# Attention scores computed two steps ahead instead of one, over three score banks, with three side banks instead of four

## The reference, cut to what matters

```
def _spatial_experts(xn, idx, in_w, in_b, out_w, out_b):
    ...
    att = jax.nn.softmax(jnp.einsum('bthd,bshd->bhts', q, k), axis=-1)
    o = jnp.einsum('bhts,bshd->bthd', att, v).reshape(B, T, D)
def _temporal_experts(xt, idx, qw, qb, kw, kb, vw, vb, pw, pb):
    ...
    logits = jnp.where(causal, logits, -jnp.inf)
    att = jax.nn.softmax(logits, axis=-1)
def _cross_mha(q_in, kv_in, in_w, in_b, out_w, out_b):
    ...
```

## Time and profile before

| | |
|---|---|
| median of 3 runs | 1999.56 us (1993.12 to 1999.69) |
| the profiled execution, its own time | 1993.96 us |
| its span, first to last instruction | 1992.2 us |
| mean granted TensorE clock | 0.977 |
| attention passes, in that span | 516 to 1712 us |

### The profile page before, as it was taken

The page is one execution under the profiler, slowest core; times in us unless marked ns, Lnnn a source line. Parts: engine busy times, 40 slices in busy tenths (PEclk is TensorE's granted clock), DMA queues, the critical chain, the costliest instruction groups (busy, mean ns, idle before and its releaser), DMA issues.

```text
span 1992.2 us, 30956 instructions
## 1 busy us (share of the span) xinstructions
PE 1824.9 (92%) x10475; PEld 1625.9 (82%) x10475; DVE 1181.7 (59%) x2333; ACT 723.5 (36%) x1345; POOL 356.4 (18%) x345
## 2 busy tenths in 40 slices
PE   1899989976899999999999899989999999999998
PEld 0678657864799989989888898879999999788996
DVE  6577558775556546563746657556656566576332
ACT  0223211013565435445544454245545444221110
POOL 3210001015121102020100002200000003455440
PEclk9999989987999999999999999999999999999999
DMA  3101000012020100011000000100000001212111
GB/s 107 32 6 43 11 6 30 8 47 94 12 115 27 32 22 11 1 69 58 11 12 11 12 1 1 38 11 12 6 8 9 6 1 44 72 36 64 43 32 52
DMA packets 25043, 60.56 MB, mean 30 GB/s; under 512 B 2548, under 2 KB 4816, under 8 KB 24149
## 3 DMA queue, kind: packets, MB, share of 16 engines
q1 hardware_dynamic: 24910, 58.74, 8.9%
HBM read 44.87 MB, written 13.86 MB: 29 GB/s over the span
## 4 chain that ended last, share of the span: by engine, by line
PE 78%; DVE 11%; issue 3%; POOL 2%; ACT 2%; DVEq 1%; DMA 1%; SPq 1%; POOLq 0%; ACTq 0%
PE ps L2273 19%; PE ps L2158 13%; PE ps L2328 7%; PE ps L1962 5%; PE ps L2255 5%; PE ps L2259 5%; PE ps L2216 5%; PE ps L2357 4%; DVE max_part L1718 4%; PE ps L2076 3%; PE ps L2042 3%; DVE share L1735 2%; PE ps L1975 2%; PE ps L2284 1%; POOL tok_b L982 1%
## 5 line engine op out<-in xcount | busy, mean ns | idle before, releaser
L2273 PE MATMUL ps<-p_raw,v_ones 125*128 125x250 f32 x2080 | 527.3, 375 | 10.5 <-DVE feat L1737 8.4
L1718 DVE TENSOR_REDUCE max_part<-ps 125x2 f32<-125x500 f32 x520 | 330.4, 674 | 246.0 <-PE ps L2216 233.7
L1294 ACT ACTIVATE p_raw<-ps 125x500 f32<-125x500 f32 x520 | 304.3, 586 | 350.9 <-PE ps L2259 346.2
L2273 PEld LDWEIGHTS ps<-p_raw,v_ones 125*128 125x128 f32 x2080 | 360.9, 190 | 37.0 <-issue 9.8
L1735 DVE RECIPROCAL share<-ps 64x250 f32<-64x250 f32 x120 | 206.3, 1719 | 79.5 <-PE ps L2273 76.6
L2255 PE MATMUL ps<-q_both_a,k_both_a 128*125 128x250 f32 x520 | 183.5, 373 | 1.8 <-ACT q_row_b L1268 1.8
L2255 PE MATMUL ps<-q_both_b,k_both_b 128*125 128x250 f32 x520 | 182.0, 371 | 0.0
L893 POOL CAST w_hi<-w_raw 128x512 fp32r<-128x512 f32 x44 | 28.1, 638 | 814.0 <-issue 359.7
L2158 PE MATMUL ps<-xa_hi,w_hi 128*128 128x418 f32 (+1 forms) x448 | 151.4, 338 | 19.8 <-POOL w_lo L895 14.0
L1559 DVE TENSOR_SCALAR onehot<-iota_h,win_key,key_t 125x320 f16 x453 | 169.1, 373 | 0.8 <-issue 0.6
L1558 DVE TENSOR_SCALAR onehot<-iota_h,low_t 125x125 f16 x453 | 127.6, 282 | 58.5 <-PE ps L2076 30.0
(11 more groups left out here) (375 smaller groups left out, 3423.4 us busy)
## 6 DMA issues: line engine op xcount, KB each, us to landing
w_raw<-in_w_mlp SPq DMA_DIRECT2D x32, 256.0 KB, 2.6
w_raw<-in_w_gps SPq DMA_DIRECT2D x16, 256.0 KB, 2.7
w_raw<-in_w_tp SPq DMA_DIRECT2D x16, 256.0 KB, 2.6
w_raw<-in_w_sp SPq DMA_DIRECT2D x12, 256.0 KB, 2.7
w_raw<-in_w_cr SPq DMA_DIRECT2D x12, 256.0 KB, 2.6
d_xt<-xb_hi SPq DMA_DIRECT2D x1, 2508.0 KB, 7.5
d_xt<-xb_lo SPq DMA_DIRECT2D x1, 2508.0 KB, 14.9
xa_hi<-d_xt SPq DMA_DIRECT2D x1, 2508.0 KB, 9.5
```

Of the source, the lines that this page charges most:

```text
L1294: act.activation(p_raw[:, g % PR, :], ps[0:TOK, g % 2, 0:4 * TOK], ACT.Exp, scale=SCALE).then_inc(s_exp, 1)
L1718: dve.tensor_reduce(part[:, y, :, j], ps[0:TOK, bank, 0:4 * TOK].rearrange("p (h k) -> p h k", h=2), AX.X, ALU.max)\
L2273: ins = pe.matmul(ps[:, bank, 0:2 * TOK], v_ones[:, n % 2, kt, h:h + 2, :], p_raw[:, g % PR, cols], start=(b == 0 and x == 0), stop=last)
```

## The change: what it does

LEAD goes from 1 to 2, so that PE has two steps of scores standing ahead of the product. The scores take banks 0, 1 and 4 in turn instead of 0 and 1, and the side tasks get banks 5 to 7 instead of 4 to 7. The due dates of R, M and Q (and of K, which hang on Q's) are one step earlier. `p_raw` keeps its three buffers.

```diff
 QR = 3
-LEAD = 1
+LEAD = 2
+S_BANK = (0, 1, 4)
 PR = 3
-SIDE_BANKS_AT = 4
+SIDE_BANKS_AT = 5
...
             gf, tasks = FIRST[n, i], maxima(n, i)
-            due["R", n, i] = gf - 4
+            due["R", n, i] = gf - 5
             for x, task in enumerate(tasks):
-                due[task] = gf - 5 - 2 * (len(tasks) - 1 - x) // 3
-            due["Q", n, i] = gf - 8 - 2 * len(tasks) // 3
+                due[task] = gf - 6 - 2 * (len(tasks) - 1 - x) // 3
+            due["Q", n, i] = gf - 9 - 2 * len(tasks) // 3
...
         if kind == "S":
-            use = [entry[1] % 2]
+            use = [S_BANK[entry[1] % 3]]
...
-                act.activation(p_raw[:, g % PR, :], ps[0:TOK, g % 2, 0:4 * TOK], ACT.Exp, scale=SCALE).then_inc(s_exp, 1)
+                act.activation(p_raw[:, g % PR, :], ps[0:TOK, S_BANK[g % 3], 0:4 * TOK], ACT.Exp, scale=SCALE).then_inc(s_exp, 1)
...
-                    to = ps[0:TOK, g % 2, 2 * TOK * x:2 * TOK * (x + 1)]
+                    to = ps[0:TOK, S_BANK[g % 3], 2 * TOK * x:2 * TOK * (x + 1)]
```

## The result

The changed kernel takes 2002.21 us (median of 13 runs, 2000.04 to 2004.74) against 1996.80 for the kernel before in the same session (13 runs, 1993.12 to 2000.35): a ratio of 1.0027, interval 1.0019 to 1.0035. That is 5.4 us slower, within the 0.5% that I had called no change. The prediction was 2000.3 us, and a change of +0.7. The 13 runs of before fall in two groups, seven from 1993.1 to 1996.8 us and six from 1998.9 to 2000.4, and the change costs 7.8 us against the median of the first and 2.7 against that of the second; the runs of after lie together.

A forecast was written before the change was run, and what follows sets the result against it. PE was taken as the bound, with 39.2 us idle in three attention stretches. Terms -2.0, -3.9, -1.6, -0.5, +5.2 and +3.5 sum to +0.7 us, on a median of 1999.56: 2000.3 us, range 1990 to 2012.

The forecast's parts named there:

- Scores two steps ahead: Attention steps: the product's wait for Exp goes, -2.0 us, and nothing more can come.
- Three side banks: Side tasks reuse banks sooner; waits come where a `unit_out` stands on DVE between, 43 new places, +3.5 us.
- with none, or with a K, V or Q in between, nothing: Places with `unit_out` between: no bank wait if the step has no M, or K, V or Q covers it.
- Rival 1: Slower: PE stops at banks behind `unit_out`, DVE falls further behind; net +14.4 or +31.6 us, deciding from +10.1; chance 0.20.
- Q and M further apart: Five places in passes 2, 6 and 7: M stands further behind its Q, 0.77 us each, -3.9 us.
- R of group 3 in passes 4 to 7: R waits about 2.2 us behind DVE's queue; +1.4 us in passes 4 to 6, +1.0 in 7, together +5.2.
- steps 199 to 203: Pass 4, likewise 5 to 7: waits only change place because DVE sets the time, 0 us; upper end 7.9 us.
- R behind its last M: R one step behind two M of its group, 33 times instead of 41, 0.2 us each: -1.6 us.
- one V: Pass 3: a V that waits up to 0.5 us for a bank finds a free one, -0.5 us.
- The clock stands at 0.99 to 1.00 in them and offers nothing.: Three attention stretches: PE's clock is near full, so only PE's idle time, 39.2 us, can be won or lost.
- The signs: Expected in PE's waits: R about 2.2 us, `max_part` at M 3 to 4 us, causal idle time near 28 us.
- "Issue" of M: M's waits called "issue", 7.6 us, held to hang on DVE: expected down by 3 to 4 us.

The follow-up runs named there:

- experiment 1: The kernel before with three side banks (5 to 7) instead of four, bank 4 unused, lead and due dates as before: 2010.53 us, ratio 1.0062.
- experiments 9 and 10: The changed kernel and the kernel before, each with `unit_out`'s reciprocal replaced by a short constant-writing instruction: 1968.27 us (0.9863) and 1973.07 us (0.9889).

## Why the prediction was right, and where it was wrong inside

The sum was +0.7 us and came to +5.4. The whole stayed within 0.5% because large terms of both signs were mis-sized together, and that is luck. So is part of the closeness of 2000.3 to 2002.21: the sum stood on 1999.56 us, and before took 1996.80 in the session of the result.

The prediction held that an order of work can win or lose PE's idle time alone. Here PE's idle time grew by 0.9 us from step 0 to step 517, and the busy time of the same matmuls by 4.6.

*Scores two steps ahead, predicted -2.0.* Measured -6.1 with the dates of before, and some -10 with the early ones. "It can't bring more: nothing else waits for the Exp" is the wrong sentence. The steps place 1.5 us more, at the ends of passes 7 and 11 and in waits that are longer by the steps than in the list.

*Three side banks, predicted +3.5.* Measured +12.6, in the order of before; **this is the term that failed.** Wrong was "with none, or with a K, V or Q in between, nothing": a linear map takes a bank as well, and so only moves the stop. The six such places in passes 9 and 10 cost 0.7 us each. Where two M stand I had 0.8 us (my own numbers, 4.95 less 4.23, give 0.7), and the waits of M in steps 162 and 172 of after are 0.70 us. Rival 1 named this mechanism; its price with "a mean of 0.3 us in 43 places", 12.9 us, is nearly what experiment 1 shows, and only the lead, which I had undervalued by 4 us, kept the change from its +10.1. In after itself, with the lead, the listed waits for `max_part` grew by no more than 3.7 us (2.0 to 5.7), about what I had forecast; in experiment 1 they grew by 6.8 us (2.0 to 8.8), half of the 12.6. The rule of the Trainium skill that I weighed (Perfetto Trace Analysis, Optimization Strategy: a repeating gap can mean too little PSUM) agrees with experiment 1, whose 0.6 and 1.0 us come at the same steps of passes 9 and 10. It doesn't say what experiments 9 and 10 point to, that the shortage is one of DVE's time: with a short `unit_out` no wait for one of the three banks is left in the list. Three banks alone with a short `unit_out` weren't run.

*Q and M further apart, predicted -3.9.* Right. In passes 5 and 6, where the Q and M of the next pass lie, the steps give -0.88 and -1.02, and -0.86 and -1.04 us: 3.8 us for the four places. The fifth, in pass 2, isn't measured by itself.

*R of group 3 in passes 4 to 7, +5.2, and steps 199 to 203, 0.* Right in the sum, less so in the split. The R waits were 1.88, 1.89, 1.90 and 0.81 us where I had 2.2. Over the ten steps from 200, 230, 260 and 290 after loses 1.6, 1.1, 1.5 and 1.9 us, 6.0 in all; with 0.9 us taken off for the clock 5.1 are left. These ten steps hold both terms, and pass 7, forecast at 1.0, lost the most.

*R behind its last M, -1.6, and one V, -0.5.* R's waits on `max_col` did shrink by 3.9 us; three of them, of 0.58 and 0.59 us, came back as the three longer waits on `q_both_b` of the last point. In passes 8 to 11, where nothing else moved, the dates bring 2.5 us with four banks, 2.5 with three, and 1.6 with three and the lead (from the table); so the term was of the right size or larger.

*"The clock stands at 0.99 to 1.00 in them and offers nothing."* Wrong as a reason: a stretch at half clock of 3.5 us is less than 0.01 in a window of 400, and it costs up to 1.6 us. But the stretches in the causal passes are worth about 1 us of after's time, so they didn't decide.

*The signs.* The R waits, the M of step 231 and the product of step 232, the 4.0 us of `max_part` at M with 0.7 us the longest, and an idle time of 27 us in the causal stretch all came nearly as written. "Issue" of M went down by 1.5 us only (7.6 to 6.1), not by 3 to 4; the rest of the gain of Q and M stood in the list as the three waits on `q_both_b` of 2.3 us that are gone. No term named the fall of the `feat` waits from 8.4 to 1.3 us, whose place the M's waits of 2.2 us took.

## What to carry to other kernels

Before a buffer is taken from a ring, look at the longest instruction of the engine that empties it, not at the mean: three banks cost 12.6 us behind a 1.72 us reciprocal, behind 0.42 us no wait for a bank was left in the list, and shortening that instruction was worth 22 us in the kernel before, four times what was at stake here (what a real division in this place could gain is less, since the short one doesn't divide, and wasn't measured). When two orders of the same work are compared, number the steps and compare their starts; the list of waits said +0.6 us, and the steps told where 5.5 went and that most of it was busy time. And a change that is two good parts and one bad one is worth taking apart: by the steps, the early dates, kept to where PE is the bound, gain some 4 us in passes 0 to 3 and 8 to 11, though the whole time of that kernel was hardly better than before's.

## What the runs showed of the hardware

The RECIPROCAL of 64 x 250 takes 1719 ns and a TENSOR_SCALAR of the same shape and source 417 ns. The Trainium skill, VectorE: DVE Perf Modes, section "Walkthrough: the 8-slice pipeline in each mode", says that the reciprocal is an iterated divide with a repeat count of 8; a ratio of 4.1 is what this case shows.

In the profile of after the granted clock fell to 1.2 GHz for some 3.5 us behind a stop of PE of 2.2 us (pass 4, 6 and 7) and once didn't behind the same 2.21 us and 1.33 us more (pass 5, all matmuls at the full rate). In the profiles with the stop filled it stayed up there, and filling only the first stop let it fall behind the second, of 1.88 us, behind which after has none. So single such stretches couldn't be told in advance from the order here, and a profile with one more or less differs by 1.6 us with no change in the code.
